# Order of the second-layer products in a mixture-of-experts 1x1 convolution: chunk by chunk, or output bank by output bank

## The reference

```python
scores = softmax(x_flat @ gate_w + gate_b)
top_v, top_i = top_k(scores, 2)
top_w = softmax(top_v)
coef = einsum('ke,kbhw->ebhw', present, wmap)      # wmap: top_w by pixel
hdn = relu(einsum('bchw,edc->ebdhw', x, w1) + b1)  # first layer, 384 -> 384
y = einsum('ebdhw,eod->ebohw', hdn, w2) + b2       # second layer, 384 -> 384
out = x_in + einsum('ebohw,ebhw->bohw', y, coef)
```

## Time and profile before

| | |
|---|---|
| median of three runs | 2469.34 us (2468.12 to 2470.34) |
| the profiled execution | 2469.91 us, of which the span from the first to the last instruction is 2468.1 us |
| TensorE matmul busy | 2449.9 us (99% of the span), 11372 matmuls |
| VectorE busy | 1413.7 us (57%) |
| ScalarE busy | 465.6 us (19%) |
| mean granted TensorE clock | 0.999 of full speed |

### The profile page before, as it was taken

How to read it: one execution, slowest core, us unless ns; L and a number is a source line. 1 busy time by engine, 2 the same in 40 slices (tenths; PEclk the granted TensorE clock), 3 DMA queues, 4 the chain that set the end, 5 groups by cost and what they waited for, 6 DMA issues and landing times.

```text
span 2468.1 us, 27782 instructions
## 1 busy us (share of the span) xinstructions
PE 2449.9 (99%) x11372; PEld 2011.4 (81%) x11372; DVE 1413.7 (57%) x2952; ACT 465.6 (19%) x777; POOL 53.3 (2%) x36
## 2 busy tenths in 40 slices
PE   7999999999999999999999999999999999999999
PEld 6788888888888888888888888888888888888887
DVE  7765556556564556545564565556556564556443
ACT  3121111111111121111111121112111111121111
POOL 0000000000000000000000000000000000000000
PEclk9999999999999999999999999999999999999999
DMA  5223122221222213111321123121221222113110
GB/s 185 90 80 104 49 90 69 94 67 49 90 92 71 67 52 123 58 69 49 113 70 69 67 77 107 49 90 69 94 67 49 90 94 68 67 51 108 54 47 26
DMA packets 127520, 189.58 MB, mean 77 GB/s; under 512 B 16032, under 2 KB 80800, under 8 KB 127392
## 3 DMA queue, kind: packets, MB, share of 16 engines
q1 hardware_dynamic: 127392, 187.80, 22.5%
HBM read 146.03 MB, written 41.75 MB: 76 GB/s over the span
## 4 chain that ended last, share of the span: by engine, by line
PE 98%; DVE 1%; DMA 1%; issue 0%; ACT 0%; POOL 0%; SPq 0%; DVEq 0%; POOLq 0%
PE z_ps L432 16%; PE y_ps L451 16%; PE y_ps L452 16%; PE y_ps L453 16%; PE z_ps L434 16%; PE z_ps L433 16%; PE g_ps L300 1%; DMA rows<-rows_dram 0%; DMA rows_dram<-wrow 0%; DMA x_raw<-in_x 0%; DVE w_lo L386 0%; DVE h_lo L490 0%; DVE x_raw L278 0%; ACT h_hi L486 0%; POOL rstd L267 0%
## 5 line engine op out<-in xcount | busy, mean ns | idle before, releaser
L479 DVE SCALAR_TENSOR_TENSOR hid<-z_ps,b_sb,rows 128x512 f32<-128x512 f32 x584 | 436.7, 748 | 896.2 <-PE z_ps L434 892.9
L451 PE MATMUL y_ps<-h_lo,w_hi 128*128 128x512 f32 x1764 | 687.6, 390 | 4.2 <-DVE h_lo L490 4.2
L452 PE MATMUL y_ps<-h_hi,w_lo 128*128 128x512 f32 x1764 | 687.0, 389 | 0.0
L453 PE MATMUL y_ps<-h_hi,w_hi 128*128 128x512 f32 x1764 | 686.9, 389 | 0.0
L432 PE MATMUL z_ps<-x_lo,w_hi 128*128 128x512 f32 x1740 | 680.8, 391 | 0.0
L434 PE MATMUL z_ps<-x_hi,w_hi 128*128 128x512 f32 x1740 | 677.5, 389 | 0.0
L433 PE MATMUL z_ps<-x_hi,w_lo 128*128 128x512 f32 x1740 | 677.0, 389 | 0.0
L486 ACT ACTIVATE h_hi<-hid 128x512 fp32r<-128x512 f32 x588 | 368.6, 631 | 1554.4 <-DVE hid L479 1549.2
L490 DVE SCALAR_TENSOR_TENSOR h_lo<-hid,h_hi 128x512 fp32r<-128x512 f32 x588 | 401.0, 682 | 5.1 <-ACT h_hi L486 4.5
L451 PEld LDWEIGHTS y_ps<-h_lo,w_hi 128*128 128x128 f32 x1764 | 331.6, 188 | 74.4 <-issue 3.1
L432 PEld LDWEIGHTS z_ps<-x_lo,w_hi 128*128 128x128 f32 x1740 | 326.6, 188 | 76.0 <-issue 9.3
(11 more groups left out here) (88 smaller groups left out, 374.3 us busy)
## 6 DMA issues: line engine op xcount, KB each, us to landing
rows<-rows_dram SPq DMA_DIRECT2D x48, 1280.0 KB, 6.1
x_raw<-in_x SPq DMA_DIRECT2D x62, 588.0 KB, 6.0
res<-in_x SPq DMA_DIRECT2D x18, 768.0 KB, 5.5
out<-res SPq DMA_DIRECT2D x17, 768.0 KB, 4.3
rows_dram<-wrow SPq DMA_DIRECT2D x32, 98.0 KB
w_in<-in_w SPq DMA_DIRECT2D x3, 576.0 KB, 9.9
res<-in_x SPq DMA_DIRECT2D x2, 744.0 KB, 4.9
out<-res SPq DMA_DIRECT2D x2, 744.0 KB, 4.1
```

Of the source, the lines that this page charges most:

```text
L451: nc.tensor.matmul(y, w2_hi[:, e, k, ms], h_lo[:, slot], start=first, stop=False)
L452: nc.tensor.matmul(y, w2_lo[:, e, k, ms], h_hi[:, slot], start=False, stop=False)
L453: ins = nc.tensor.matmul(y, w2_hi[:, e, k, ms], h_hi[:, slot], start=False, stop=last)
L479: nc.vector.scalar_tensor_tensor(hid[:, q % HIDS], z_ps[:, q % ZB], b1_sb[:, e, k:k + 1], coef, ALU.add, ALU.mult).then_inc(scaled, 1)
```

## The change

The two loops of `mm2` change places. The outer loop goes over the banks m, the inner one over the chunks k; all nine products of a bank follow one another. The wait for a chunk's `hlo_ready` is taken the first time that the unit needs the chunk, which is in bank 0. The wait for `out_ready` stands ahead of each bank's nine. In the last unit `tail_product` is incremented by the last of each bank's nine products. The number of matmuls, their operands and the number of waits stay as they are.

```diff
-            for k in range(NK):
-                slot = (NK * u + k) % RING
-                pe.wait_ge(hlo_ready, NK * u + k + 1)
-                for m in range(NJ):
-                    y = y_ps[:, m]
-                    ms = slice(m * P, (m + 1) * P)
+            for m in range(NJ):
+                y = y_ps[:, m]
+                ms = slice(m * P, (m + 1) * P)
+                if e == 0 and t:
+                    pe.wait_ge(out_ready, t * NJ - NJ + m + 1)
+                for k in range(NK):
+                    slot = (NK * u + k) % RING
+                    if m == 0:
+                        pe.wait_ge(hlo_ready, NK * u + k + 1)
                     first, last = e == 0 and k == 0, e == E - 1 and k == NK - 1
-                    if first and t:
-                        pe.wait_ge(out_ready, t * NJ - NJ + m + 1)
                     nc.tensor.matmul(y, w2_hi[:, e, k, ms], h_lo[:, slot], start=first, stop=False)
                     nc.tensor.matmul(y, w2_lo[:, e, k, ms], h_hi[:, slot], start=False, stop=False)
                     ins = nc.tensor.matmul(y, w2_hi[:, e, k, ms], h_hi[:, slot], start=False, stop=last)
-                    if tail and k == NK - 1:
-                        ins.then_inc(tail_product, 1)
+                if tail:
+                    ins.then_inc(tail_product, 1)
             if not tail:
                 ins.then_inc(unit_done, 1)
```

## The result

The changed kernel takes 2474.23 us in the median of 20 runs (2470.90 to 2476.04), the kernel before beside it 2469.56 us (2467.85 to 2471.12, 20 runs). The ratio is 1.0016, 95% interval [1.0011, 1.0022], that is 2.7 to 5.4 us more: a small loss, 0.16% by the middle of the interval. The median lies inside the range that was given, 1.1 us above the forecast. The profiled execution (2471.49 us, span 2469.7) is one of the faster ones.

What follows compares the result with a forecast made beforehand. TensorE's matmul stream was taken as the bound, busy for 2449.9 of 2468.1 us. The terms 2.72 - 0.11 + 1.2 = 3.8 us gave 2473.7 for the profiled execution and 2473.1 for the median, range 2470.8 to 2475.4.

Steps and rivals of the forecast that it cites:

- The rate: TensorE's steady matmul stream: nine products in a row to a bank change nothing; zero, bound 2.0 us either side.
- Unit 3: Start-up wait for the third `h_lo`: 21 matmuls instead of 9 stand behind it, 2.72 us later.
- the `out_ready` step: Ahead of unit 4's second layer: the small step for bank 0's `out_ready` goes, -0.11 us.
- Unit 2: Start-up: a new 1.67 us wait for the third `h_lo`, which only shortens unit 3's wait and adds nothing.
- Unit 0: First start-up unit: no new wait at half clock, so zero; 1.0 us later at full clock, kept for the range.
- the prediction's own signs of being wrong: Included unit 3's third `h_lo` being itself later, meaning unit 0 or 1 had pushed image 1's gate product.
- The clock: After unit 3's longer idle time, TensorE may run a stretch at half clock; 1.2 us taken, up to 1.5.
- The slower rival: Granted clock falls more than once on the path or stays low for a second stretch; 2474.9 us, chance 0.17.
- The end: Last unit: banks 0 and 1 finish sooner, but bank 2's last matmul and sum stay last; zero.

Runs made afterwards that it cites:

- late units alone: Against the kernel before, bank by bank only in units 5 to 195; its profile is the changed kernel's pair; 2468.72 us against 2469.34, ratio 0.9999.
- fill3: Changed kernel plus 12 extra matmuls, results unused, in unit 3's wait for its third `h_lo`; 2472.47 us against 2469.34 for the kernel before.
- the kernel with `h_lo` first: Kernel before, but VectorE makes tile 0's last `h_lo` ahead of tile 1's first `scale`; 2468.96 us against 2469.34, ratio 0.9997.

## Why the prediction was right, point by point

**The rate: right.** Zero was taken for nine products in a row to a bank; the stretch from unit 5 to unit 195 agrees to 0.01 us in 2360.67, far inside the bound of 2.0, and the late units alone gave 0.9999. The Trainium skill ("TensorE: Matmul & The Clock Gate", section on psum-queue depth-cycling) tells of a kernel that cycles through PSUM banks, idles briefly between its groups of matmuls and loses throughput by the clock. As a rule for this kernel it would have let the change gain by fewer changes of bank; this case's traces don't agree, with 2360.67 us for nine products in a row to a bank and 2360.68 for three.

**Unit 3: right.** 2.72 us were given for 12 more matmuls behind the third `h_lo`; 2.73 were measured from restart to next first layer, 2.57 more from unit 1 to unit 5 against its pair, where 2.61 stood in the sum with the `out_ready` step. Unit 3 changed alone costs about the whole loss, though with more of the clock in it. TensorE went on at 76.20 and not at 77.0, because this execution ran unit 0 at the upper clock.

**Unit 2: right.** A wait of 1.46 us came, about the size given, and costs nothing beside unit 3's, by the 22.07 us with and without it.

**Unit 0: mis-sized.** The step took zero, because the profiled execution ran that unit at half clock, where the earlier needs are just met, and kept 1.0 us for the range. Both sizes are right for their clock. The start of unit 1 before, and the starts of units 0 and 1 in fill3, whose unit 0 has the changed order and fell to half clock too:

```profile
44.77 0.39 PE L451 MATMUL y_ps<-h_lo,w_hi 128*128 128x512 f32 x1
```

```profile
34.71 0.77 PE L459 MATMUL y_ps<-h_lo,w_hi 128*128 128x512 f32 x1 [2.17 <-DVE h_lo L498]
...
44.51 0.39 PE L459 MATMUL y_ps<-h_lo,w_hi 128*128 128x512 f32 x1
```

At half clock unit 0 takes 44.77 - 34.95 = 9.82 us in the old order and 44.51 - 34.71 = 9.80 in the new; at full clock it is 8.26 and 9.24, 0.98 longer. Whether the clock falls in unit 0 differs from run to run; a term that leans on it should have been weighed over both. And one of the prediction's own signs of being wrong came with it: unit 3's third `h_lo` is itself later, TensorE going on at 76.20 in place of 74.99 in the pair, and the gate product with it. Unit 2's wait can't push that chain, unit 0 can.

**The clock: right in kind, its size open.** 1.2 us were taken for half clock after unit 3's longer wait. The profiled execution had none after 3.16 us idle, and no profile here shows one after just that wait. Over the runs, filling it gives 1.0 us and leaves none at a mean clock of 0.998, so it very likely occurs. But the kernel before also loses 1.2 us to half clock, against 1.7 for the changed one in all, so by the middle of these figures the change adds 0.4 by the clock. From the spread of the runs this difference of differences has a standard error of about 0.6 (an estimate), so 1.2 is not excluded. Together, 3.6 to 3.7 us without the clock and 0.4 with it come to the 4.1 by which the means of the 20 runs differ (the medians differ by 4.7); 3.8 was forecast. By these figures two terms were off, unit 0's too low and the clock's too high, by about as much; that they cancel is luck. The slower rival, more than one stretch on the path, had 0.17; it does occur, since 8 of the 20 runs lie over 0.2% above the median before, but it doesn't decide the median.

**The end: right.** The timeline of VectorE, the last of the three sums in the changed kernel:

```profile
2466.49 0.75 DVE L509 SCALAR_TENSOR_TENSOR res<-y_ps,bias,res 128x512 f32<-128x512 f32 x1 [1.29 <-PE y_ps L454]
```

It ended at 2467.24, 1.17 us after the last matmul's start; before, the three ended at 2465.56, 1.22 after it. The earlier sums of banks 0 and 1 bought next to nothing.

What was not foreseen is a part of the reason itself: the prediction named the DMA of rows as the cause of unit 3's late `h_lo`, and so it is, but VectorE's sums for unit 4 come late behind it too, as the kernel with `h_lo` first showed.

## What to carry to other kernels

Changing which loop is outside moves when each input is first needed, even if the work stays the same. Read from the trace the margin of the latest input at its new place, in the steady stream and, apart from it, in the start-up, where a wait of the old order may already sit on the path: work that stood ahead of that wait now stands behind it, and costs its full length. And look for what makes that input late before reordering around it; here a DMA of its own for the first 0.26 MB of 1.28 won 3.1 us, where the change had cost 4.7.

## What the runs showed of the hardware

After a wait TensorE's granted clock may fall to 0.50, the lower level of 1.2 GHz, and whether it does is not fixed by the idle time alone. 2.10 us idle was followed by it in unit 0 of the kernel before and not in unit 3. 3.16 us idle in the changed kernel's unit 3 was not; 4.81 us in the kernel with unit 3 alone was, and there it lasted 6.2 us. The 1.86 us in unit 4 of the kernel with `h_lo` first was, though TensorE had run without a gap for 6 us ahead of it, and there the clock fell only 1.2 us after TensorE had gone on. Matmuls that compute nothing, put into the waits, kept the mean clock at 1.000 in all 22 runs of the two kernels that had them in every wait. The changed kernel's spread was 5.1 us in 20 runs and, so filled, 2.1 in 11.
